# A mixture of experts whose weighted rows are summed by the scatter: three sums in DRAM in place of six rows a token

## The reference, cut to what matters

```python
E, M, K, C = 64, 176, 6, 96                      # experts, width, choices a token, rows an expert
scores = softmax(x @ gate.T)                     # then only the best 3 of 8 groups
topk_w, topk_i = top_k(tmp_scores, K)
pos  = (number of earlier choices of the same expert)
slot = topk_i * C + minimum(pos, C - 1)          # all choices past 95 share the last row
buf  = zeros(E * C, H).at[slot].set(x[tok])      # the last writer keeps the shared row
out  = (silu(buf @ Wg.T) * (buf @ Wu.T)) @ Wd.T  # for each expert
y    = sum(out[slot] * topk_w, axis=1)           # six weighted rows a token
result = x + y + shared(x)
```

## Time and profile before

| | us |
|---|---|
| median of three timed executions | 1605.34 (1599.73 to 1607.7) |
| the profiled execution, its own time | 1592.39 |
| its span, first to last instruction | 1590.4 |
| TensorE busy | 1382.2 (87%) |
| VectorE busy | 1121.4 (71%) |
| ScalarE busy | 676.9 (43%) |
| GpSimd busy | 737.9 (46%) |

### The profile page before, as it was taken

One profiled execution on the slowest core, in us unless ns is written; L12 is line 12 of the kernel. 1 busy time (PEld: TensorE's weight loads), 2 busy tenths in 40 slices (PEclk: granted clock), 3 DMA queues, 4 the chain that ended last, 5 costly groups with the idle time before them and its releaser, 6 DMA issues. The chain is left out here.

```text
span 1590.4 us, 35813 instructions
## 1 busy us (share of the span) xinstructions
PE 1382.2 (87%) x13732; PEld 971.8 (61%) x13733; DVE 1121.4 (71%) x2131; ACT 676.9 (43%) x1430; POOL 737.9 (46%) x811
## 2 busy tenths in 40 slices
PE   3849999997679999999999999999986976999832
PEld 2424545445546777777777777777765545888731
DVE  4867888876767898788878887887764687222229
ACT  1226777772144555555555555555541110222200
POOL 0341111100338697667666766676650027677610
PEclk9968999999779999999999999999997888999965
DMA  3052000000116988788788887887783300799838
GB/s 107 1 233 86 2 2 2 2 2 1 54 51 126 160 154 142 142 152 152 140 137 155 146 145 135 157 142 145 136 151 109 92 1 15 232 281 281 256 121 266
DMA packets 423530, 191.39 MB, mean 120 GB/s; under 512 B 377507, under 2 KB 397697, under 8 KB 423249
## 3 DMA queue, kind: packets, MB, share of 16 engines
q1 hardware_dynamic: 404576, 164.08, 49.1%
q0 software_dynamic: 6144, 12.52, 2.7%
q10 hardware_dynamic: 12656, 12.72, 2.5%
HBM read 73.91 MB, written 23.13 MB: 61 GB/s over the span
## 5 line engine op out<-in xcount | busy, mean ns | idle before, releaser
L941 POOL CAST a_ph<-a_p 128x1024 f16<-128x1024 f32 (+7 forms) x256 | 248.8, 972 | 232.4 <-ACT a_p L1087 232.3
L1137 DVE TENSOR_TENSOR a_ph<-a_p,a_ph 128x1024 f16<-128x1024 f32 (+7 forms) x256 | 259.6, 1014 | 14.5 <-POOL a_ph L941 14.4
L1087 ACT ACTIVATE a_p<-bank,a_negm 128x1024 f32<-128x1024 f32 (+7 forms) x256 | 188.9, 738 | 125.3 <-DVE a_negm L1154 124.9
L1047 PE MATMUL bank<-a_v,a_pt 128*128 128x128 f16 x3456 | 234.8, 219 | 4.6 <-DMA a_pt<-a_ph 4.4
L1029 PE MATMUL bank<-a_k,a_q 128*128 128x512 f16 (+3 forms) x1152 | 229.1, 326 | 7.8 <-ACT a_p L1087 7.1
L1047 PEld LDWEIGHTS bank<-a_v,a_pt 128*128 128x128 f16 x3456 | 211.0, 98 | 36.1 <-issue 3.5
L1154 DVE TENSOR_REDUCE a_negm<-bank 128x1 f32<-128x1024 f32 (+7 forms) x256 | 189.9, 742 | 25.7 <-PE bank L1034 24.1
L972 PE MATMUL bank<-x_part,wsplit 128*128 128x512 f16 x768 | 189.1, 384 | 1.8 <-PEq L182 1.8
L686 ACT ACTIVATE a_p<-bank 128x1024 f32<-128x1024 f32 x192 | 152.9, 809 | 68.0 <-PE bank L571 57.1
L1029 PEld LDWEIGHTS bank<-a_k,a_q 128*128 128x128 f16 x1152 | 98.8, 98 | 69.0 <-ACT a_p L1087 8.9
L706 DVE TENSOR_REDUCE a_max<-bank 128x2 f32<-128x1024 f32 (+3 forms) x128 | 128.8, 1022 | 17.0 <-PE bank L571 14.5
(11 more groups left out here) (206 smaller groups left out, 2441.5 us busy)
## 6 DMA issues: line engine op xcount, KB each, us to landing
wgu<-in_wgu SPq DMA_DIRECT2D x64, 352.0 KB
choice_rows<-zero SPq DMA_DIRECT2D x24, 512.0 KB, 5.8
wh<-in_wqkv SPq DMA_DIRECT2D x32, 384.0 KB, 3.9
c_rows<-choice_rows ACTq DMA_DIRECT2D x16, 768.0 KB
wd<-in_wd SPq DMA_DIRECT2D x64, 176.0 KB
a_pt<-a_ph SPq DMA_TRANSPOSE x256, 3.8
x<-in_x SPq DMA_DIRECT2D x1, 2048.0 KB, 9.3
wo<-in_wo SPq DMA_DIRECT2D x1, 2048.0 KB, 10.1
```

The costliest lines, as they stand in the source:

```text
L941: pool.tensor_copy(halves[j][:, :, 0, :], probs[j % 2][:, 0:blocks[j] * P].rearrange("p (n q) -> p n q", q=P)).then_inc(h_ready, 1)
L1047: ins = pe.matmul(V_ps[j % 2][:, 0:DH1], turned[j][:, 2 * q + a, :], vs[n % 2][v_][:, q, :], start=(q == 0 and (a, v_) == PARTS[0]), stop= ...
L1087: act.activation(probs[j % 2][:, 0:w_], S_ps[j % 2].rearrange("p a n -> p (a n)")[:, 0:w_], ACT.Exp, bias=negm[:, n % 2, j:j + 1], accum_o ...
L1137: dve.tensor_tensor(halves[j][:, :, 1, :], probs[j % 2][:, 0:blocks[j] * P].rearrange("p (n q) -> p n q", q=P), halves[j][:, :, 0, :], ALU ...
```

## The change

It does seven things, all from the router on but for the zeros.

1. `choice_rows` with 12288 rows is replaced by three arrays `sum_rows0` to `sum_rows2` of 2304 rows (2048 tokens and 256 spare rows). They are zeroed in the first attention, 7.1 MB in place of 12.6.
2. The scatter adds to its destination in DRAM (`compute_op=ALU.add`); expert e adds into sum e mod 3, and waits first for the scatter of e - 3. A slot without a choice adds to a spare row of its own, where it was left out before.
3. The weight is applied where ScalarE copies the result out of PSUM. For this the router stores each token's weights behind its row in `token_rows` (264 numbers a row in place of 256), the gather brings them along, and VectorE picks the right one with a mask (`choice_mask`) by a multiplication and a reduction for every pair of experts.
4. The first eight gathers are issued by GpSimd at the end of the router's block.
5. The loop is written out for all 64 experts. The weights are 11 experts ahead in place of 8, the gathered rows are awaited by pairs, with eight buffers in both versions.
6. combine reads three rows a token: 12 loads of 512 KB on two queues, GpSimd adds two of the three sums, VectorE the rest, in groups of four tiles.
7. Semaphores of the norms are shared, and a buffer of the router takes the place of another. GpSimd waits for the zeros in the feed-forward stage, far ahead.

```diff
-XB = 8
+XB = 11
+XR = 8
 XG = 4
+NR = 2
...
+            sp.wait_ge(s_wk, 1)
+            sp.dma_start(g.xrows.rearrange("(n p) d -> p n d", p=P)[:, :, D:D + 8], g.wk[:, :, :]).then_inc(s_wkst, 16)
...
-            pool.wait_ge(g.s_zero, 16 * ZD)
+
+            pool.wait_ge(s_wkst, 16)
+            pool.wait_ge(s_src, 1)
+            for e in range(XR):
+                gather_rows(g, pool, e)
...
+def gather_rows(g, pool, e):
+
+    pool.indirect_dma_start(out=g.rows[:, e % XR, :], out_offset=None, in_=g.xrows,
+                            in_offset=bass.IndirectOffsetOnAxis(ap=g.src[:, e:e + 1], axis=0),
+                            bounds_check=T - 1, oob_is_err=False).then_inc(g.s_row[e // 2 % (XR // 2)], 16)
...
             for e in range(E):
-                if e + XB < E:
+                if e + XR < E:
 
                     pool.wait_ge(s_t, e // 2 + 1)
-                    gather(e + XB)
-                pool.wait_ge(s_o, e + 3)
-                pool.indirect_dma_start(out=g.krows, out_offset=bass.IndirectOffsetOnAxis(
-                    ap=g.dst[:, e:e + 1], axis=0), in_=orow[e % XB // XG][:, e % XG, :], in_offset=None,
-                    bounds_check=K * T - 1, oob_is_err=False).then_inc(s_scat[e % XB // XG], 16)
+                    pool.wait_ge(s_ws, e // 2 + 1)
+                    gather_rows(g, pool, e + XR)
+                if e >= NA:
+
+                    pool.wait_ge(s_scat[e % NA], 16 * (e // NA))
...
+                pool.wait_ge(s_o, e + 1)
+                pool.indirect_dma_start(out=g.sums[e % NA], out_offset=bass.IndirectOffsetOnAxis(
+                    ap=g.dst[:, e:e + 1], axis=0), in_=orow[e // XG % NR][:, e % XG, :], in_offset=None,
+                    bounds_check=TA - 1, oob_is_err=True, compute_op=ALU.add).then_inc(s_scat[e % NA], 16)
...
+            def turn_pair(j):
+
+                pe.wait_ge(g.s_row[j % (XR // 2)], 32 * (j // (XR // 2) + 1))
...
+                act.wait_ge(s_ws, e // 2 + 1)
+                act.activation(orow[q % NR][:, e % XG, :], g.bank[2][0:C, e % 2, 0:D], ACT.Copy,
+                               scale=weight[:, e:e + 1]).then_inc(s_o, 1)
...
+                dve.tensor_tensor(wtmp[:, :, :], rows[:, 2 * j % XR:2 * j % XR + 2, D:D + 8],
+                                  g.km[:, 2 * j:2 * j + 2, :], ALU.mult).then_inc(s_wp, 1)
+                dve.wait_ge(s_wp, j + 1)
+                dve.tensor_reduce(weight[:, 2 * j:2 * j + 2], wtmp[:, :, :], AX.X, ALU.add).then_inc(s_ws, 1)
...
+            for i in range(NC):
+                pool.wait_ge(s_g[i][1], two_in[i])
+                pool.tensor_tensor(rows[i][:, 1, :, :], rows[i][:, 1, :, :], rows[i][:, 2, :, :],
+                                   ALU.add).then_inc(s_two, 1)
...
+            for i in range(0, NC, 2):
+                for a in (1, 2, 0):
+                    sp.dma_start(rows[i][:, a, :, :], sv[a][:, CT * i:CT * i + CT, :]).then_inc(s_g[i][a], 16)
```

More of the change, by code:

```diff
@@ L54 @@
 OOB = 65536
-ZD = 24
+NA = 3
+TA = T + 256
+ZD = 6 * NA
 def constants():
@@ L72, in constants @@
     token = np.arange(T, dtype=np.float32).reshape(NT, P).T
-    last = np.where(np.arange(P) == C - 1, OOB, -T).astype(np.float32)[:, None]
+    last = np.zeros((P, 10), np.float32)
+    last[:, 0] = T + np.arange(P)
+    last[:, 1] = np.arange(P) != C - 1
+    last[C - 1, 9] = 1.0
     return {"c_rope": np.ascontiguousarray(rope), "c_ident": ident, "c_mask": np.ascontiguousarray(masks),
@@ L740, in _ @@
             def _(sp):
-                zv = g.krows.rearrange("(z p n) d -> z p (n d)", p=P, z=ZD)
-                for z in range(ZD):
-                    sp.dma_start(zv[z], g.zero[:, :]).then_inc(g.s_zero, 16)
+                for a in range(NA):
+                    zv = g.sums[a].rearrange("(z p n) d -> z p (n d)", p=P, z=ZD // NA)
+                    for z in range(ZD // NA):
+                        sp.dma_start(zv[z], g.zero[:, :]).then_inc(g.s_zero, 16)
 WS = 4
@@ L1656, in _ @@
         @block.gpsimd
         def _(pool):
-            def gather(e):
-                pool.indirect_dma_start(out=rows[e % XB // XG][:, e % XG, :], out_offset=None, in_=g.xrows,
-                                        in_offset=bass.IndirectOffsetOnAxis(ap=g.src[:, e:e + 1], axis=0),
-                                        bounds_check=T - 1, oob_is_err=False).then_inc(s_row[e % XB // XG], 16)
-            for e in range(XB):
-                gather(e)
             for e in range(E):
-                if e + XB < E:
+                if e + XR < E:
@@ L1736, in _ @@
-            with pe.Fori(0, E // XB - 1) as i:
-                one_pass(i, True)
-            one_pass(E // XB - 1, False)
-        def walk(eng, step_turn, step_expert, step_down):
-            step_turn(0, 0)
-            step_expert(0, 0)
-            def one_pass(i, more):
-                for s in range(XB):
-                    if s % 2 == 0 and (more or s + 2 < XB):
-                        step_turn(i * (XB // 2) + (s // 2 + 1), (s + 2) % XB)
-                    if more or s + 1 < XB:
-                        step_expert(i * XB + (s + 1), (s + 1) % XB)
-                    step_down(i, i * XB + s, s)
-            with eng.Fori(0, E // XB - 1) as i:
-                one_pass(i, True)
-            one_pass(E // XB - 1, False)
+            turn_pair(0)
@@ L1757, in _ @@
+            gu(0)
+            for e in range(E):
+                if e % 2 == 0 and e + 2 < E:
+                    turn_pair(e // 2 + 1)
+                if e + 1 < E:
+                    gu(e + 1)
+                down(e)
         @block.scalar
         def _(act):
-            act.nop().then_inc(s_o, 2)
-            for i in range(NR):
-                act.nop().then_inc(s_out[i], 16)
-            act.nop().then_inc(s_free, NR)
-            def silu(e, s):
-                act.wait_ge(s_gu, e + 5)
-                act.wait_ge(s_h, e + 1)
-                act.activation(sg[s % 2][:, :, :], g.bank[1][0:MH, s % 2, 0:2 * C].rearrange(
-                    "p (m c) -> p m c", c=C), ACT.Silu).then_inc(s_sil, 1)
@@ new lines, in product @@
+            def product(e):
+                dve.wait_ge(s_sil, e + 1)
+                if e >= 2:
+                    dve.wait_ge(s_dn, e - 1)
+                dve.tensor_tensor(h[e % 2][:, :, :], g.bank[1][0:MH, e % 2, 2 * C:4 * C].rearrange(
+                    "p (m c) -> p m c", c=C), sg[e % 2][:, :, :], ALU.mult).then_inc(s_h, 1)
+            turned(0)
+            product(0)
+            for e in range(E):
+                if e % 2 == 0 and e + 2 < E:
+                    turned(e // 2 + 1)
+                if e + 1 < E:
+                    product(e + 1)
@@ L1810, in combine @@
 def combine(nc, g, c, out):
-    NB = 8
-    rows = [g.sb(f"c_rows{i}", [P, K, D], F32, c) for i in range(NB)]
+    CT = 4
+    NC = NT // CT
+    rows = [g.sb(f"c_rows{i}", [P, NA, CT, D], F32, c) for i in range(NC)]
     last = g.sb("c_last", [E, D], F32, c)
-    s_g = g.s_wgu
-    EXPERTS = 32 * (E // XB)
-    s_acc, s_st, s_l, s_mm = g.sem("c_acc"), g.sem("c_store"), g.sem("c_last"), g.sem("c_mm")
+    s_g = [[g.s_wgu[NC * min(a, 1) + i] for a in range(NA)] for i in range(NC)]
+    one_in = [32 * len(range(i, E, XB)) + 16 for i in range(NC)]
@@ L1819, in combine @@
+    two_in = [32 * len(range(i, E, XB)) + 32 for i in range(NC, 2 * NC)]
+    s_one, s_full, s_two, s_bank, s_acc, s_st, s_l, s_mm = [g.sem(f"c_{n}") for n in ("one", "full", "two", "bank", "acc", "store", "last", "mm")]
     ov = out.rearrange("b (n p) d -> p (b n) d", p=P)
-    kv = g.krows.rearrange("(k n p) d -> p n k d", n=NT, p=P)
-    STEPS = K + 1
+    sv = [g.sums[a][0:T, :].rearrange("(n p) d -> p n d", p=P) for a in range(NA)]
     with nc.Block() as block:
```

280 lines of the change are left out of this document (147 added, 133 removed).

## The result

The changed kernel takes **1590.66 us** (median of 12 runs, 1585.9 to 1593.19), the kernel before beside it 1604.45 (12 runs, 1596.64 to 1613.25). The ratio is 0.9914, 95% interval 0.9894 to 0.9933: 13.8 us, 0.9%, faster. That lies in the predicted range and on the predicted side, 8.7 us above the value of 1582. So the two traces differ by only 6.3 us of span, and the medians by 13.8. In which stage the other 7.5 us lie, no trace shows. The table splits the two traces; a turn is the time from one scatter to the next.

What follows compares the result with a forecast made beforehand. GpSimd's issue time was taken to bound the experts, DMA engines close behind. Last stage -25.9, start +3.0, experts +0.6, tail -1.7, landing +1.0 gave a 1567.4 span; taken off the timed median, 1582 us, range 1566 to 1608.

Steps and rivals of the forecast that it cites:

- the likeliest case: The forecast without any rival coming true: 1571 to 1592 us, given a chance of 0.50.
- The experts, +0.6 predicted: Experts' loop: 2.64 us from scatter to scatter, as before, so 55 experts take 0.6 us more.
- rival 2: Experts: an accumulating scatter costs GpSimd 1.42 us to issue instead of 0.95; +20 us, 1602; chance 0.14.
- TensorE's 13.6 us of waits should mostly go: Experts: rows awaited by pairs, eight buffers deep, should remove most of TensorE's 13.6 us of waiting for gathered rows.
- The DMA engines' price of adding: Experts: reading the destination rows in DRAM costs the DMA engines 0.33 us more per accumulating scatter.
- rival 3: Experts: the DMA engines add at half speed, 0.33 us more per scatter; +21 us, 1603; chance 0.12.
- The ring, no wait predicted: Experts: three sums taking turns leave 7.0 us for a scatter to land; 5.6 assumed, so no wait.
- Rival 1: Experts: waiting for the scatter three earlier sets the pace, 3.38 us a turn; +45 us, 1627; chance 0.14.
- The tail, -1.7 predicted: Last eight experts, which have no gather: 17.0 us in place of 18.7, without row waits.
- The start, +3.0 predicted: Router's end to experts: gathers moved ahead put a stage's end behind them, so TensorE starts 3.0 us later.
- Rival 4: Router's end: GpSimd's DRAIN costs its 10.5 us in full; +9.8 us, 1592; chance 0.10.
- The last stage, -25.9 predicted: Combining stage: half the bytes and 96 weighted additions removed, loads become the bound; 25.9 us less, bounds 22 and 28.

Runs made afterwards that it cites:

- plain_scatter: The changed kernel with the addition taken out of the scatter, so rows are plainly written to the same three arrays: 1571.6 us, ratio to before 0.9791.
- before_adding: The kernel before with only its scatter into choice_rows made to add instead of overwrite: 1621.0 us, ratio to before 1.0114.
- light_weights: The changed kernel loading only 16 of 128 partitions of the gate and up weights of experts from 11 on: 1589.4 us, one execution.
- two_sums: The changed kernel with two sums in place of three and no GpSimd addition in the last stage: 1609.4 us, one execution.
- half_rows: The changed kernel with 48 of the 96 rows in each accumulating scatter: 1593.0 us, one execution.
- gathers_late: The changed kernel with the first eight gathers put back to the start of the experts' block: 1588.9 us, ratio to before 0.9906.
- c_last_early: The changed kernel with only the load of c_last moved from the last stage to the end of the experts' block: 1591.5 us, ratio to before 0.9942.

## Why the prediction was right, and where its terms were off

The side and the range held; the mechanism held in one half. The last stage gives most of what was forecast. But the experts, put at nothing, take all of it: -22.1 and +22.3 in the traces. What the traces have left, 6.3 us, comes from the tail (-5.0) and the DRAIN (-4.4), which the sum had at -1.7 and 0. That these two traces still show the changed kernel faster is luck in part, and by the prediction's own sign ("I'm wrong ... if its scatter takes over 1.1") the likeliest case had failed. Of its other signs, the last stage (31.8, 28 said), VectorE's time in it (16.8, under 16 said), TensorE's waits, the DMA share and the DRAIN after the experts were off as well.

In the span, where the sum was made, 1567.4 stood for 1584.1, 16.7 too low: experts +21.7, last stage +3.8, against tail -3.3, DRAIN -4.4 and start -1.1. In the medians only 8.7 of this shows. The sum was taken off a median that lay 13 above the profiled execution of before, and after's lies only 5 above its own: luck too.

- **The experts, +0.6 predicted, +22.3 measured.** The step that failed is "GpSimd: a pair is still one gather and one scatter, 2.53". The adding scatter takes 1.44 us of GpSimd for the 0.95 counted, which makes 3.03. It is rival 2 that happened, at almost its price (1.42 guessed; turn 3.0, 3.035 measured); plain_scatter and before_adding show it from both sides. The price was a guess, by counting pieces, and no run shows that pieces are the reason: a close hit by luck. Rival 2 gave 1602, and the time is 11 below it: 3 are the other terms, the rest is the place of the two profiled executions among their runs. I had given it 0.14 and written why it would be natural; the rows had nothing on an adding scatter, and a cost that no row shows was put at zero in the likeliest case. The Trainium skill (Perfetto Trace Analysis, DMA Instruction — SWDGE), cited there, ends such a record with the last descriptor; the trace agrees in that a scatter's record ends 4.0 us (median) before it lands. What GpSimd does in the added 0.49 us no run shows.
- **"TensorE's 13.6 us of waits should mostly go"**: they grew to 22.0. A slower GpSimd hands out rows later. They don't matter, as GpSimd paces everything. GpSimd's own waits, the 5.4 us of the sum, did go.
- **The DMA engines' price of adding, 0.33 us assumed.** The share of 0.93 over a turn of 3.035 is 2.82 us of their work per expert, the upper bound that I gave. In plain_scatter, whose row for the same piece (first scatter to last gather) stands below, 0.95 over 2.67 is 2.53, so adding costs them 0.29; the same working on before_adding (0.90 over 3.19) and before (0.92 over 2.63) gives 0.45. The 0.33 was about right, and the 0.66 of rival 3 is not reached. light_weights shows that it bound nothing here, so rival 3 fell; "DMA share at or above 1.0" was wrong.

```profile
1365.80:1512.37 146.57, 135.75 (x1238) 118.01 (x1237) 42.68 (x141) 44.68 (x113) 106.42 (x110) 1.00 0.95 271
```

- **The ring, no wait predicted**: right. Behind the end of the issue, as the sum counted, the landing took 4.0 us in the median and at most 5.9, against 5.6 assumed and 7.0 of room. Rival 1 fell; two_sums shows that it stands one sum away.
- **The tail, -1.7 predicted, -5.0 measured.** The last scatters now follow each other by GpSimd's own pace, 13.7 / 8 = 1.72 us (1.41 and the gap of 0.30), where before they came at TensorE's, 18.7 / 8 = 2.34: GpSimd had fallen behind, and TensorE's results lay ready. Part of the experts' loss is given back here.
- **The DRAIN after the experts, unchanged in the sum, 4.4 shorter.** Not foreseen. It goes with the adding (plain_scatter 9.85, before_adding 6.59 for 10.51), but half_rows adds too and has 9.85; the cause stays open.
- **The start, +3.0 predicted, +1.9 measured.** The step was right: with the gathers ahead of it the router's end waits for GpSimd. The DRAIN ended 2.1 us after the last issue, where the sum had 2.3 (1.6 for the landing and 0.7), and TensorE began at 1352.7 for 1352.9. Rival 4, the full 10.5, fell. VectorE's mask additions ended at 1342.6, before 1346 as said. What I did not price is the alternative: gathers_late shows that moving the gathers cost 3 us.
- **The last stage, -25.9 predicted, -22.1 measured.** The loads did land where the sum had them (near 1574.0, 21.7 us in). "VectorE is then no bound" failed: 16.8 us of work that can hardly begin before the first rows, slowed by GpSimd's additions beside it, leave five additions where I had counted one. From the last landing to the end are 10.1 us, 6.5 in the sum. (The 45.7 and 43.4 us of the 96 old additions were misread: they overlap and take 38.6, and 43.4 is the stage with the 16 from PSUM. Nothing in the sum hung on it.) That the late c_last was the cause, my first theory after the result, fell with c_last_early.

## What to carry to other kernels

An indirect DMA that GpSimd issues costs its engine nearly a fixed time per instruction and little per row (1.4 to 2.4 ns here): fill it (128 rows rather than 96), and where GpSimd is the pace, count its instructions before its bytes. Letting the DMA do arithmetic is not free to the engine that issues it; when an attribute of an instruction has no row, run the old kernel with that attribute alone, one line, before building on it. When traffic halves, the stage's bound changes owner: ask what the next engine can have done by the time the last byte lands.
